# Two attention layers with a routed expert layer between them: expert results scattered to token order and added by plain accumulating loads, and router rows normalised once in a ring of three with late second scatters

## The reference, cut to what matters

```python
# x: (64, 128, 128); 64 sequences of 128 tokens of width 128, 8192 tokens in all
x = x + cross_attention_0(layernorm(x), side input of 128 keys and context of 120 keys)   # 16 heads of 8
h = layernorm(x).reshape(8192, 128)
logits = small_attention_over_experts(h @ wqkv.T)             # (8192, 8)
top_logits, idx = top_k(logits, 2); scores = softmax(top_logits)
x = x + sum over k in 0, 1 of scores[:, k] * expert[idx[:, k]](h)
    # expert e: (silu(h @ a_e) * (h @ g_e)) @ w2_e, inner width 352
x = x + cross_attention_1(layernorm(x), context of 120 keys)
x = x + adapter mixture of 8 rank-64 experts (top 2, gelu) of layernorm(x)
```

## Time and profile before

| | |
|---|---|
| median of three runs | 1629.61 us |
| lowest, highest | 1625.89, 1629.79 us |
| span of the profiled execution | 1619.5 us |
| PE busy | 1352.2 us, 83% of the span |
| DVE busy | 1128.8 us, 70% |
| POOL busy | 984.3 us, 61% |
| ACT busy | 873.4 us, 54% |
| mean granted PE clock | 0.926 |

### The profile page before, as it was taken

How to read it: one execution, slowest core, us unless ns; L and a number is a source line. 1 busy time by engine, 2 the same in 40 slices (tenths; PEclk the granted TensorE clock), 3 DMA queues, 4 the chain that set the end, 5 groups by cost and what they waited for, 6 DMA issues and landing times. The chain is left out here.

```text
span 1619.5 us, 46602 instructions
## 1 busy us (share of the span) xinstructions
PE 1352.2 (83%) x16805; PEld 1116.4 (69%) x16805; DVE 1128.8 (70%) x3395; ACT 873.4 (54%) x1634; POOL 984.3 (61%) x1122
## 2 busy tenths in 40 slices
PE   1689899898999988199999992369898889959999
PEld 0368677777777777199999991157676767747777
DVE  5779877787888885456555553368887888647776
ACT  1267666666766657066666660145565566624444
POOL 4447678777788866544444444888888886012221
PEclk9799999899999999599999995689999999969999
DMA  6667766666666642322222223678888787221221
GB/s 179 191 185 230 211 202 184 181 184 184 210 192 181 212 133 86 122 62 66 65 65 64 64 63 91 162 186 218 219 223 229 218 219 220 77 65 66 78 71 53
DMA packets 197816, 239.32 MB, mean 148 GB/s; under 512 B 39281, under 2 KB 165105, under 8 KB 190433
## 3 DMA queue, kind: packets, MB, share of 16 engines
q1 hardware_dynamic: 164608, 209.51, 42.5%
q0 software_dynamic: 26848, 25.91, 7.6%
q10 hardware_dynamic: 6144, 1.06, 0.4%
HBM read 148.34 MB, written 87.00 MB: 145 GB/s over the span
## 5 line engine op out<-in xcount | busy, mean ns | idle before, releaser
L701 DVE TENSOR_REDUCE L_neg_max<-L_ps_mx 128x2 f32<-128x496 f32 (+1 forms) x768 | 492.1, 659 | 140.0 <-PE L_ps_mx L851 136.5
L580 ACT ACTIVATE L_p<-L_ps_sc 120x512 f32<-120x512 f32 (+1 forms) x768 | 419.3, 598 | 228.3 <-PE L_ps_sc L838 225.7
L851 PE MATMUL L_ps_mx<-stack_k,stack_q 118*128 118x248 bf16 (+1 forms) x2048 | 303.3, 252 | 53.2 <-DMA stack_q<-L_q_rows 27.7
L838 PE MATMUL L_ps_sc<-stack_q,stack_k 122*120 122x128 bf16 (+1 forms) x3072 | 303.0, 223 | 6.1 <-DMA stack_q<-L_mT 4.7
L838 PEld LDWEIGHTS L_ps_sc<-stack_q,stack_k 122*120 122x120 bf16 (+1 forms) x3072 | 243.8, 124 | 69.0 <-issue 39.9
L428 POOL DMA_INDIRECT L_x<-routed_out,route_slots_all x128 | 200.9, 1570 | 49.0 <-issue 31.5
L871 PE MATMUL L_ps_o<-L_p,L_v 120*9 120x128 f32 (+1 forms) x6144 | 225.5, 281 | 3.3 <-ACT L_o_sb L607 2.7
L851 PEld LDWEIGHTS L_ps_mx<-stack_k,stack_q 118*128 118x128 bf16 x2048 | 149.7, 101 | 102.5 <-DVE L_neg_max L701 42.1
L871 PEld LDWEIGHTS L_ps_o<-L_p,L_v 120*9 120x9 f32 (+1 forms) x6144 | 145.8, 92 | 43.2 <-issue 25.3
L1436 DVE TENSOR_TENSOR M_hT<-M_act_a,M_ps_g 128x384 f32<-128x384 f32 x135 | 74.8, 554 | 126.3 <-ACT M_act_a L1396 120.4
L1344 POOL COPY M_w<-stack_q 128x384 f32 x135 | 69.1, 512 | 144.2 <-PE M_ps_y L1377 138.0
(11 more groups left out here) (193 smaller groups left out, 2432.1 us busy)
## 6 DMA issues: line engine op xcount, KB each, us to landing
L_q_rows<-L_q_parts_sb SPq DMA_DIRECT2D x192, 192.0 KB
stack_q<-L_q_rows SPq DMA_DIRECT2D x192, 192.0 KB
stack_k<-L_k_rows SPq DMA_DIRECT2D x96, 372.0 KB
stack_k<-L_k_rows SPq DMA_DIRECT2D x96, 180.0 KB
L_k_rows<-L_k_parts_sb SPq DMA_DIRECT2D x32, 372.0 KB
M_x<-routed_in SPq DMA_DIRECT2D x135, 66.0 KB, 1.8
routed_out<-M_y POOLq DMA_DIRECT2D x135, 64.0 KB
x<-L_out SPq DMA_DIRECT2D x32, 256.0 KB, 3.6
```

Source lines behind the costliest of these rows:

```text
L580: nc.scalar.activation(p_t[t][u % 2][:, quarter * 4 * S:(quarter + 1) * 4 * S], ps_sc[n % NSC][0:KEYS[t], :], ACT.Exp).then_inc(sc_read, 1)
L701: nc.vector.tensor_reduce(neg_max[:, b, kk * HPB:(kk + 1) * HPB], v, AX.X, ALU.max, negate=True).then_inc(max_read, 1)
L838: last = mm(ps_sc[n % NSC][0:KEYS[t], j * S:(j + 1) * S], k_st[p][:, b // 2, h, b % 2, k0:k0 + KEYS[t]], q_st[p][:, b // 2, h, b % 2], sta ...
L851: last = mm(ps_mx[i % NMX][:, j * NK:(j + 1) * NK], q_st[p][0:TERM_TOP, b // 2, h, b % 2], k_st[p][0:TERM_TOP, b // 2, h, b % 2], start=Tr ...
```

## The change

1. **Where expert results go.** Each routed row now carries, beside its gate, the row of `routed_out` for which its result is meant: group, choice k, partition and sequence, in that order. POOL stores a tile's results by an indirect scatter to these rows. Rows that only fill up a tile carry a row of a dump area behind the tokens'; for this `route.zeros` grows from 128 x 132 to 128 x 16 x 132 numbers with its column of row numbers. Since the scatter reads the row numbers out of the loaded tile, SP's load into a buffer now waits until the result of the tile that used it has been stored (`y_stored`), no longer only until it was computed.
2. **How layer 1 reads them.** The eight gathers of a group become two plain accumulating DMAs of 256 KB each from consecutive rows. The table of all slots and the four DVE instructions ahead of the first expert tile go.
3. **The router's rows.** A group is normalised once, into a ring of three buffers without the k dimension. The gate and row number for the second choice are kept in `second`; once the first scatter has landed, `regate` on DVE (unit 1, after the second maximum) copies them into the row columns, and then the second scatter goes out from the same rows. The second scatter of group g-4 is now the first thing on POOL in step g, ahead of the K split; the router's normalising moves ahead of the first scatter, and bias add to the end. For the last group DVE still fills a second buffer.

```diff
-            def gather(g4, first_one, last_one):
+            def add_routed(g4, k):
...
-                for b, k in [(b, k) for k in range(TOP) for b in range(GB)][first_one:last_one]:
-                    nc.gpsimd.indirect_dma_start(
-                        out=x_t[g4.n % NX][:, b], out_offset=None, in_=ys,
-                        in_offset=bass.IndirectOffsetOnAxis(ap=route.slots_all[:, g4.n, b, k:k + 1], axis=0),
-                        compute_op=ALU.add).then_inc(gathered[k][g4.par], 16)
+                rows = bass.ts(g4.n * TOP + k, S * GB)
+                pool.dma_start(x_t[g4.n % NX][:], ys[rows].rearrange("(s b) d -> s b d", b=GB),
+                               accum_op=ALU.add).then_inc(routed_added[k][g4.par], 16)
...
                 if first:
+                    if (g + -4).exists:
+                        rt.scatter(pool, g + -4, 1)
                     if later:
...
-                    late = g.n < NG
+                    if (g + -1).exists:
+                        rt.deviation(pool, g + -1)
+                        if g.n < NG:
+                            rt.normalise(pool, nc.gpsimd, g + -1, 0)
                     if g.n <= NG and (g + -3).exists:
                         rt.scatter(pool, g + -3, 0)
-                    if g.n == NG:
-                        rt.scatter(pool, g + -3, 1)
-                    if g.exists:
-
-                        pool.wait_ge(normed, g.n + 1)
-                        r = x_t[g.n % NX]
-                        nc.gpsimd.tensor_tensor(r[:], r[:], bo_bc[:].unsqueeze(1).to_broadcast([S, GB, D]),
-                                                ALU.add).then_inc(res_ready, 1)
-                    if (g + -1).exists:
-                        rt.deviation(pool, g + -1)
-                    if (g + -1).exists and late:
-                        rt.normalise(pool, nc.gpsimd, g + -1, 0)
-                    if late and (g + -3).exists:
-                        rt.scatter(pool, g + -3, 1)
...
-                    if (g + -2).exists and g.n >= NG:
+                    if g.n == NG:
+                        rt.scatter(pool, g + -2, 0)
+                    if g.n == NG + 1:
+                        rt.scatter(pool, g + -3, 1)
                         for k in range(TOP):
                             rt.scatter(pool, g + -2, k)
-                    if (g + -1).exists and late:
-                        rt.normalise(pool, nc.gpsimd, g + -1, 1)
...
-                    gather(g + 4, 0, GB)
+                    add_routed(g + 4, 0)
...
-                    gather(g + 4, GB, GB * TOP)
+                    add_routed(g + 4, 1)
...
+    def rows(self, g, k):
+        return (g.n + 1) % RING if k and g.n == NG - 1 else g.n % RING
...
+    def regate(self, dve, g, part):
+        i = self.rows(g, 0)
+        dve.wait_ge(self.scattered[i][0], self.scatters_of(i, 0, g.n + 1))
+        self.nc.vector.tensor_copy(self.xn[i][:, :, D:D + GATE_COLUMNS], self.second[g.par][:]).then_inc(self.regated, 1)
...
-    (1, 2): (2, Router.form_logits, 1), (2, 0): (2, Router.form_logits, 2), (2, 2): (2, Router.pick, 0),
+    (1, 1): (4, Router.regate, 0), (1, 2): (2, Router.form_logits, 1), (2, 0): (2, Router.form_logits, 2), (2, 2): (2, Router.pick, 0),
...
-                    wait(sp, y_ready, tl - NX + 1)
+                    if has(tl - NX):
+                        sp.wait_ge(y_stored[(tl - NX) % NY], ((tl - NX) // NY + 1) * 16)
...
-                    pool.dma_start(ys[ts * S:(ts + 1) * S], y_t[ts % NY][:]).then_inc(y_stored[ts % NY], 16)
+                    token_row = x_t[ts % NX][:, D + 1:D + 2].bitcast(mybir.dt.uint32)
+                    nc.gpsimd.indirect_dma_start(
+                        out=ys, out_offset=bass.IndirectOffsetOnAxis(ap=token_row, axis=0),
+                        in_=y_t[ts % NY][:], in_offset=None).then_inc(y_stored[ts % NY], 16)
...
-            link(v.tensor_tensor(crossed[:], slots_f[:].unsqueeze(2).to_broadcast(each),
-                                 region0[:, 1:E].unsqueeze(1).to_broadcast(each), ALU.is_ge))
-            link(v.tensor_tensor(crossed[:], crossed[:], route.delta[:, 0:E - 1].unsqueeze(1).to_broadcast(each), ALU.mult))
-            link(v.tensor_reduce(moved[:], crossed[:], AX.X, ALU.add))
-            link(v.tensor_tensor(slots_all[:].rearrange("s n b k -> s (n b k)"), slots_f[:], moved[:], ALU.subtract))
```

More of the change, by code:

```diff
@@ L215, in attention_layer @@
         if not first:
-            gathered = [two(lambda p: sem(f"gathered{p}{k}")) for k in range(TOP)]
+            routed_added = [two(lambda p: sem(f"routed_added{p}{k}")) for k in range(TOP)]
         k_written = sem("k_written")
@@ L296, in zero_end_rows @@
                     row = sp.value_load(route.end_row[0:1, e:e + 1], min_val=e * REGION, max_val=e * REGION + TOKENS)
-                    sp.dma_start(route.xs[bass.ds(row, S)], route.zeros[:]).then_inc(route.zeroed, 16)
+                    sp.dma_start(route.xs[bass.ds(row, S)], route.zeros[:, e]).then_inc(route.zeroed, 16)
             def step(g):
@@ L516, in _ @@
             if first:
-                for p in range(2):
-                    nc.gpsimd.memset(rt.xn[p][:, :, :, D:ROW], 0.0)
+                for rows in rt.xn:
+                    nc.gpsimd.memset(rows[:, :, D:ROW], 0.0)
                 fill_rest(0)
@@ L751, in between @@
                         stage(rt, dve, g + -behind, part)
+                if first and (g.n, u, k) == (NG + 1, 2, 1):
+                    rt.regate(dve, g + -3, 0)
+                if first and (g.n, u, k) == (NG + 1, 5, 3):
+                    rt.normalise(dve, nc.vector, g + -2, 1)
             def step(g):
@@ L942, in _ @@
             done(nc.gpsimd.tensor_copy(route.iota_t[:], route.iota_ti[:]))
+            done(nc.gpsimd.iota(route.row_i[:], pattern=[[S * GB, TOP], [1, GB]], base=0, channel_multiplier=GB))
             done(nc.gpsimd.memset(route.zeros[:], 0.0))
+            done(nc.gpsimd.iota(route.zeros[:, :, D + 1].bitcast(I32), pattern=[[S, 2 * E]], base=TOKENS * TOP,
+                                channel_multiplier=1))
         @block.vector
@@ L991, in __init__ @@
         self.stats, self.mv, self.rstd = sb("stats", [S, GB, 6]), sb("mv", [S, GB, 2]), sb("rstd", [S, GB])
-        self.xn = two(lambda p: sb(f"xn{p}", [S, TOP, GB, ROW]))
+        self.xn = [sb(f"xn{i}", [S, GB, ROW]) for i in range(RING)]
+        self.second = two(lambda p: sb(f"second{p}", [S, GB, 2]))
         self.xnT, self.qkv = sb("xnT", [D, GB * S]), sb("qkv", [S, GB, 3 * E])
@@ L1030, in statistics @@
             wait_apart(dve, self.stats_ready, (g.n + 1) * GB, self.passed)
-            wait(dve, self.copied, g.n)
+            wait(dve, self.normed, g.n)
             for b in range(GB):
@@ L1123, in form_slots @@
             self.after(dve, g, "slots")
[L1124 to L1127 removed]
+            second = self.second[g.par][:]
+            first = self.xn[self.rows(g, 0)][:, :, D:D + GATE_COLUMNS]
+            v.tensor_copy(first[:, :, 0], self.g0[:])
+            v.tensor_tensor(second[:, :, 0], self.e2[:], self.g0[:], ALU.mult)
+            for k, columns in enumerate((first, second)):
+                v.tensor_scalar(columns[:, :, 1].bitcast(I32), self.route.row_i[:, k], float(g.n * TOP * GB * S), None, ALU.add)
+            v.tensor_copy(self.slot[g.n % RING][:], self.slot_f[:]).then_inc(self.slot_ready, 1)
     def tile_table(self, dve):
@@ L1180, in fill @@
             for b in range(GB):
-                last = self.nc.tensor.transpose(misc[:, b * S:(b + 1) * S], self.xn[g.par][:, 0, b, 0:D], self.route.ident[:])
+                last = self.nc.tensor.transpose(misc[:, b * S:(b + 1) * S], self.xn[self.rows(g, 0)][:, b, 0:D], self.route.ident[:])
         elif name == "RQ":
@@ L1202, in deviation @@
     def deviation(self, pool, g):
-        wait(pool, self.copied, g.n)
+        wait(pool, self.normed, g.n)
         wait_apart(pool, self.aggregated, g.n + 1, self.passed)
```

76 lines of the change are left out of this document (40 added, 36 removed).

## The result

The changed kernel takes 1617.04 us (median of 17 runs, 1601.57 to 1626.32), the kernel before on the same chip 1629.61 (17 runs): a ratio of 0.9918, 95% interval 0.9894 to 0.9941. It is faster, by 0.8% or some 13 us, where 42 were forecast. The time lies inside the stated range, 1532 to 1624 us, but by luck: it was drawn to take in dear loads, and the case that came in part, slowed experts, was said to be left out. The profiled executions have spans of 1619.5 us before and 1620.8 after. A run's time is 1.6 to 1.7 us more than its span here, so the profile of before should lie about 8 us under the median of its runs, and that of after lies 5 us over, and the two spans show no gain. They do show where time went and came from, which the runs without a trace can't.

A forecast was written before the change was run, and what follows sets the result against it. Experts and layer 0 bound by PE, layer 1 by POOL's gathers: +2.3 start, -4 + 22 + 2 layer 0, -0.8 + 1.2 joints, -26 - 39 layer 1 = -42.3 us, giving 1587 us; range 1532 to 1624.

The forecast's parts named there:

- dear loads: Layer 1, rival: accumulating loads cost POOL 6.3 us each, so the kernel takes 1618 us; chance 0.10.
- the sentence that weighed "DMA: Bandwidth & Descriptors": Layer 1's start: the skill's rule lands 256 KB in 2.6 us against 3.5 estimated, gaining 2 to 4 us more.
- Hidden, by 1 us only: Experts: the load's wait for stored results takes 5.4 us, while PE needs the buffer only after 6.4.
- the third rival: Experts become bound by stored results: 2.5 us per tile, +50 us, 1638 us in all; chance 0.12.
- Layer 0's steps: Layer 0, ten steps: 39.8 us each against 37.6, +22 us; bounds 38 (+4) and 41.2 (+36).
- The waits for `stack_q`: Layer 0: PE newly waits 3 to 5 us for the stacks at the start of steps 5 to 14.
- the R+34.9 of the forecast: Layer 0: PE ready for its next step 34.9 us after step start R, including a 2.2 us hole at RX.
- The hole at RX: Layer 0: PE still waits for POOL's normalised rows in each full step, near 2 us.
- The end of layer 0: POOL's last scatters at layer 0's end: +2 us, between -3 and +6.
- layer 0 keeps to PE's pace: Layer 0, rival: stacks land within 12 us of the query split, so the kernel takes 1538 us; chance 0.18.
- the removed normalising shows nothing: Layer 0, rival counted within the forecast: the dropped 3.13 us normalising on POOL is not on the path; no separate chance.
- Theory A's forecasts: Layer 0, late second scatter: steps of 35 to 36 us, about 1562 us; with eight expert buffers about 1540.

The follow-up runs named there:

- run 4: Changed kernel with eight input buffers for the experts instead of six: ratio 0.9701 to the kernel before, experts 291.1 us.
- run 10: Changed kernel with eight input buffers for the experts, again on another chip: ratio 0.9718 to the kernel before, experts 291.1 us.
- run 2: Kernel before with only the router's ring, regate and second scatter at the step's head; results stored and gathered as before: ratio 1.0151, experts 290.9 us.
- Run 1: Kernel before with only results scattered to token order and plain accumulating loads, router's order as before: ratio 0.969, experts 320.7 us.
- run 5: Changed kernel unaltered, repeated on a slower chip: ratio 0.9788 to the kernel before, 1659.57 us, experts 321.2 us.
- run 8: Changed kernel with each tile's result stored by a plain DMA instead of the indirect scatter (wrong results): ratio 0.9769 to the kernel before, experts 299.4 us.
- run 11: Changed kernel with eight expert buffers, a ring of four and the second scatter at the end of POOL's step: ratio 0.9606 to the kernel before.
- the late order: Changed kernel with second scatter moved behind the first and a ring of four: ratio 0.9977 to the kernel before; 0.9807 with eight expert buffers.
- run 3: Changed kernel with the second scatter behind the first scatter and a ring of four: ratio 0.9977 to the kernel before, layer 0 steps 44.1 us.
- run 6: Changed kernel with the second scatter behind the first, a ring of four and eight expert buffers: ratio 0.9807 to the kernel before, steps 44.4 us.

## Why the forecast was wrong, point by point

- *Layer 1* was right in sign, place and size: the start -26.5 us (-26 forecast), steps of 20.2 (20.2), POOL busy 135 of 300 us in full steps. The two adds of group 0 take from 1050.67 to 1059.93, 9.3 us, where 9 to 10 were put. That is 4.4 and 4.9 us each from issue to what waits for it, so the sentence that weighed "DMA: Bandwidth & Descriptors" of the Trainium skill is decided: its rule, fitted to DMAs issued by POOL, gives 2.6 us for 256 KB, and the measurement holds.
- *The step that failed first*: "Hidden, by 1 us only". The experts lost 27.7 us. This was the third rival in its mechanism, at a price between none and its 50. Its sum of 5.4 us takes one landing of 1.5 us and one load of 1.8 for all tiles. In the trace a load is issued 3.2 us (median of 129) after the start of the scatter it waits for, 2.2 after the issue's end, where 1.65 was put (1.5 and 0.15): half of the 1 us of slack is gone in the typical tile. Then both terms vary. In 18 tiles the load is issued more than 4.0 us after the scatter's start, at most 5.3. And in 15 tiles it is the load that is slow, 2.6 to 3.9 us from its issue to the weight load that waited for it; these cost more, 15.7 of the 24.4 us that the weight loads wait from tile 6 on. Runs 4 and 10 show the cause, the load's wait for stored results at six buffers, and run 2 that without part 1 there is no loss.
- *What makes a landing late* was in no theory, but the traces point at something. The profile lists a DMA queue called "instruction"; in the experts' stage after it moves 21 packets of 16 KB, 0.9 to 1.7 us each. Such a packet overlaps all 15 slow loads and all 18 late scatters, but only 21 of the other 111 scatters. Run 1 has the same 15 of 15 and 13 of 13, run 5 16 of 17 and 17 of 18. In run 8, where every load's landing is on record, the 23 loads beside such a packet land in 2.44 us (median), at most 3.4, the other 112 in 1.84. Before, they do no harm (22 packets, no wait after the start but one of 1.0 us). No run changed the packets, so this is a coincidence in time, not a proof.
- *Layer 0's steps* were right in mechanism as far as this one trace shows, low in size: 41.4 us against 39.8, +32.8 instead of +22. In step 9 `regate` comes at R+9.1 where R+7.0 was put, with 1 us for the low clock; the rest of the chain up to the Q split, 16.3 us, was forecast at 15.9; the stacks took 16.3 us where 14.8 to 17.3 were seen. The upper bound of 41.2 was in the text and nearly hit. The waits for `stack_q` appeared, 25.2 us over nine full steps, 2.8 each instead of 3 to 5. So PE itself was ready for the next step about 4 us later than the R+34.9 of the forecast, which had put DVE's part at nothing: two of DVE's instructions lose 3.8 us a step, and PE's waits for DVE's maxima rise by 21 us over the nine steps. With the stacks early the step would have been some 39 us long even so, by this subtraction, and no run on this chip tests it. The hole at RX, which should have stayed at 2 us, is gone: PE comes later than POOL.
- *The end of layer 0*: +5.8 us, at the bound of +6. At 695.17 POOL has waited 2.39 us for `regate`, and from 698.00 on it issues its last fifteen scatters in one row, where before they ran from 660.60 on.
- *Rivals*: that layer 0 keeps to PE's pace didn't come about; an adding load costs 0.92 us, not 6.3; "the removed normalising shows nothing" is borne out by run 11.
- With the measured sizes the sum is -2.6 + 32.8 + 5.8 + 0.7 + 27.7 - 63.0 = +1.4, the difference of the two spans. The medians differ by -12.6; how the other 14 us spread over the stages no trace shows.
- Theory A's forecasts for the late order (runs 3 and 6) were mine too, and fell: I had read the steps of a chip without the stalls. Whether the late order pays on the chip of the result wasn't tried.
- Open: what stops the engines beside the scatters on the three slower chips, and how layer 0's loss divides between stalls, DVE's long instructions and late stacks, there and on the chip of the result.

## What to carry to other kernels

When a buffer's release moves from "computed" to "stored", count the slack against the late landings of the trace, of the store and of the load, not against the typical ones, and buy it with buffers: with two more of 68 KB the experts took 291 us, where six took 305 to 321 with the scatter. A DMA block that waits for another engine does not belong at the head of an in-order queue whose later work feeds a transfer chain; what it delays comes back as a wait a step later. And change one thing at a time: on the slower chips the half of this change that pays was worth 4.9% with enough buffers, and the half meant to spare one POOL pass took 2 points of it.

## What the runs showed of the hardware

- Three chips ran the kernel before 3.0 to 3.7% slower than the fourth. There ACT, DVE and PE stop, mostly for 1 to 5 us, at most for 8.7 (run 6), with no releaser on the core, mostly beside POOL's indirect scatters; with eight scatters in a row such pieces come to 182 and 192 us in nine steps (runs 3 and 6), with four to 62 to 104. On the chip of the result no such wait is listed before or after.
- A tiny DVE instruction beside POOL's instructions can last until they end: 2.26 us (over two of POOL's) and 1.96 (over one) instead of 0.16 and 0.23. The Trainium skill has this in "SBUF — State Buffer", Who interferes with whom: the port pair that the two share is an exclusive lock; a DVE instruction with two inputs in SBUF contends for it with a POOL instruction that reads SBUF, and so does a copy or cast in a two-port mode, where the one that comes second is fully blocked. The trace agrees with a lock, for a cast and a two-input addition; whether this cast ran in a two-port mode no run shows, and that it waited through two POOL instructions the page doesn't say.
- An accumulating plain load of 256 KB took POOL 0.92 us to issue and 5.4 us (median of 32) to land while layer 1 ran at 240 GB/s.
- Nearly all loads and scatters of the experts that landed late in the changed kernel overlapped a 16 KB packet of the queue that the profile calls "instruction". In run 8 a load of 66 KB beside one took 2.44 us (median), the others 1.84.
